# Second expert layer of a decoder: dense experts over all tokens, or each routed expert over its own rows

## The reference, cut to what matters

```python
gates = softmax(x @ router_w); idx1 = argmax(gates); idx2 = argmax(gates * (1 - mask1))
pos1 = cumsum(mask1) - mask1;                 mask1 *= pos1 < capacity
pos2 = cumsum(mask2) - mask2 + sum(mask1);    mask2 *= pos2 < capacity
g1, g2 = g1 / max(g1 + g2, eps), g2 / max(g1 + g2, eps)
expert_in = einsum('nec,nh->ech', dispatch, x)          # 560 rows for each of 8 experts
hmid = silu(einsum('ech,ehf->ecf', expert_in, w1) + b1)  # 128 -> 512
expert_out = einsum('ecf,efh->ech', hmid, w2) + b2       # 512 -> 128
y = einsum('nec,ech->nh', combine, expert_out)
out = y + 0.1 * (silu(x @ sw1 + sb1) @ sw2 + sb2)
```

## Time and profile before

| | us |
|---|---|
| median of 3 runs | 1636.73 |
| profiled execution, first to last instruction (span) | 1638.0 |
| last stage, from its first load to the end | 1428.1 to 1638.0 |
| nine experts' matmuls, first to last | 1437.4 to 1633.7 |

### The profile page before, as it was taken

The page is one execution under the profiler, slowest core; times in us unless marked ns, Lnnn a source line. Parts: engine busy times, 40 slices in busy tenths (PEclk is TensorE's granted clock), DMA queues, the critical chain, the costliest instruction groups (busy, mean ns, idle before and its releaser), DMA issues. The chain is left out here.

```text
span 1638.0 us, 45036 instructions
## 1 busy us (share of the span) xinstructions
PE 1531.2 (93%) x16356; PEld 1187.5 (72%) x16356; DVE 1108.0 (68%) x1746; ACT 897.3 (55%) x1421; POOL 705.6 (43%) x757
## 2 busy tenths in 40 slices
PE   8988999989999987789999999999999999889998
PEld 4445676679989655467777777777777777678887
DVE  4334545677787468467777777777777777367777
ACT  5454332432222347346666666666666666567776
POOL 2200000577877456443444433444433444066665
PEclk9779999999999999799999999999999999989999
DMA  2064984131110000466655556655556654212211
GB/s 78 21 171 122 241 253 120 39 127 42 64 42 23 0 2 2 104 153 153 151 131 130 130 135 150 150 126 130 128 141 150 145 127 112 56 42 75 75 60 45
DMA packets 55699, 169.74 MB, mean 104 GB/s; under 512 B 13761, under 2 KB 27425, under 8 KB 55617
## 3 DMA queue, kind: packets, MB, share of 16 engines
q1 hardware_dynamic: 52928, 156.83, 38.4%
q10 hardware_dynamic: 2688, 11.78, 2.4%
HBM read 90.80 MB, written 1.29 MB: 56 GB/s over the span
## 5 line engine op out<-in xcount | busy, mean ns | idle before, releaser
L1993 DVE TENSOR_REDUCE hat_tops<-banks 128x1 f32<-128x500 f32 x672 | 441.8, 676 | 151.6 <-PE banks L1738 151.4
L1866 ACT ACTIVATE hat_pb<-banks 125x896 f32<-125x896 f32 x384 | 340.2, 916 | 226.7 <-PE banks L1757 222.5
L1738 PE MATMUL banks<-hat_kh,hat_qm 128*128 128x500 f32 x672 | 298.4, 461 | 3.7 <-DVE hat_tops L1993 3.4
L1757 PEld LDWEIGHTS banks<-hat_q,hat_k 128*125 128x125 f32 x1536 | 219.3, 188 | 74.9 <-issue 32.6
L1757 PE MATMUL banks<-hat_q,hat_k 128*125 128x224 f32 x1536 | 250.3, 286 | 16.4 <-ACT hat_pb L1866 9.1
L1935 POOL CAST hat_kh<-hat_kf 128x500 fp32r<-128x500 f32 x96 | 58.3, 607 | 403.6 <-ACT hat_kf L1879 389.3
L1748 PE MATMUL banks<-hat_pb,hat_vs 125*27 125x168 f32 (+1 forms) x6144 | 166.9, 261 | 0.1
L1748 PEld LDWEIGHTS banks<-hat_pb,hat_vs 125*27 125x27 f32 (+1 forms) x6144 | 132.0, 98 | 44.1 <-issue 24.4
L1311 ACT ACTIVATE ffn_rg<-banks 128x448 f32<-128x448 f32 x128 | 69.7, 545 | 164.4 <-PE banks L1244 164.3
L1738 PEld LDWEIGHTS banks<-hat_kh,hat_qm 128*128 128x128 f32 x672 | 127.5, 191 | 41.0 <-DVE hat_tops L1993 25.5
L2247 DVE TENSOR_TENSOR moe_hl<-moe_hf,moe_hh 128x448 fp32r<-128x448 f32 x128 | 108.5, 887 | 42.2 <-POOL moe_hh L2139 41.5
(11 more groups left out here) (293 smaller groups left out, 3055.8 us busy)
## 6 DMA issues: line engine op xcount, KB each, us to landing
hat_k<-hat_kh SPq DMA_DIRECT2D x256, 187.5 KB, 4.7
hat_ct<-ctxT SPq DMA_DIRECT2D x32, 750.0 KB, 6.2
hat_k<-hat_kl SPq DMA_DIRECT2D x128, 187.5 KB, 4.5
ctx_cx<-ctx SPq DMA_DIRECT2D x32, 672.0 KB
ctx_cd<-ctxT ACTq DMA_DIRECT2D x15, 750.0 KB, 5.4
ffn_cb<-expert_weights SPq DMA_DIRECT2D x8, 896.0 KB, 4.4
moe_cb<-expert_weights SPq DMA_DIRECT2D x8, 896.0 KB, 6.6
moe_raw<-Mw SPq DMA_DIRECT2D x18, 256.0 KB, 3.0
```

Source lines behind the costliest of these rows:

```text
L1738: peak_out.inc(nc.tensor.matmul(g.bank(PK + m % 2)[:, 0:SB], qm[u][:].rearrange("p h i -> p (h i)")[:, r * 128:r * 128 + 128], kh[u][:, c ...
L1757: mm = nc.tensor.matmul(g.bank(2 * (t % 2) + j // 2)[0:SW, (j % 2) * QW:(j % 2 + 1) * QW], k3[u][:, j, t * SW:(t + 1) * SW], q3[u][:, j, : ...
L1866: exped.inc(nc.scalar.activation(pb[t % 6][:].rearrange("p (n i) -> p n i", n=2), g.ps[0:SW, 2 * (t % 2):2 * (t % 2) + 2, 0:2 * QW], ACT.E ...
L1993: peaked.inc(v.tensor_reduce(tops[:, r, n:n + 1], g.bank(PK + m % 2)[:, 0:SB], AX_X, ALU.max))
```

## The change

`experts_silu` and its helper go; `experts1` is written anew. SLOTS = 8 x 560 = 4480 rows of XW = 130 words (128 features, one word for the token's number, one spare) lie in DRAM (`slot_rows`), and 2 x 1792 rows of 128 (`token_rows`) for the results. Both are cleared by SP in the first block of the causal attention.

- The normalized tokens are turned to rows (14 transposes on PE), kept by ACT, doubled by POOL for the second choice, and given their numbers. `Route` works out the slot of each token and choice on DVE; each of 2 x 14 tiles of 128 rows is sent to its slots by an indirect DMA issued on POOL.
- Meanwhile the shared expert runs over all tokens as before, with a ring of 6 tiles and a lag of 4; POOL makes its first four remainders, DVE the other twelve, after it has worked out the slots. DVE adds a tenth of its output to `xt` (`mix`).
- SP loads the 560 rows of an expert, PE turns them (`turn`), ACT and DVE split them, and the expert runs over 4 tiles of 560 columns, each as two halves of 280 (6 matmuls up, 6 down). DVE adds the bias, PE turns the result back (`turn_out`), and POOL sends it to its tokens by 5 indirect DMAs of 112 rows (`send`), whose indices lie in the rows that came (`rows`, three buffers). Six sets of split weights are kept, made by POOL, for three of them by ACT and DVE.
- At the end SP loads both results of each token, PE sums them with matmuls against diagonal matrices of the shares (`lots`), and DVE adds them to `xt`.

```diff
+SLOTS = E * CAPACITY
+XW = D + 2
@@ causal_attention, first block
+            @block.sync
+            def _(sp):
+                sp.wait_ge(emptied, 2)
+                sp.dma_start(g.slot_rows.rearrange("(n p) c -> p n c", p=128), spread(g.empty[:], 1, SLOTS // 128)).then_inc(cleared, 16)
+                sp.dma_start(g.token_rows.rearrange("(n p) c -> p n c", p=128), spread(g.empty[:, 0:D], 1, 2 * TT)).then_inc(cleared, 16)
+                sp.wait_ge(cleared, 32)
...
+                nc.gpsimd.memset(g.empty[:, 0:D], 0.0).then_inc(emptied, 1)
+                nc.gpsimd.memset(g.empty[:, D:XW], 1.0).then_inc(emptied, 1)
@@ Route(Choice)
+    def take(self, dve, k):
+        self.candidates(dve, k, (self.sc, self.rest)[k])
+        self.step(dve, v.tensor_reduce(self.row[:, 7, :], self.tmp[:], AX_X, ALU.max))
+        v.tensor_tensor(self.hot[:, k], self.tmp[:], self.wide(7), ALU.is_equal).then_inc((self.one, self.two)[k], 1)
...
+    def place(self, dve, bank, k):
+        dve.wait_ge(self.tallied, k + 1)
...
+        for n in (1, 2, 4, 8):
+            v.tensor_copy(b[:, 0:n], a[:, 0:n]).then_inc(self.stepped, 1)
+            v.tensor_tensor(b[:, n:TT], a[:, n:TT], a[:, 0:TT - n], ALU.add).then_inc(self.stepped, 1)
...
+        v.tensor_scalar(self.slot[:, k], self.row[:, 4, :], float(SLOTS), None, ALU.add).then_inc(self.slotted, 1)
@@ experts1, SP
+                    if s == SETS - 1:
+                        sp.wait_ge(sent_all, 16 * 2 * TT)
+                        for e in range(3):
+                            sp.dma_start(rows[e][:], g.slot_rows[...]).then_inc(rows_in[e], 16)
+                for e in range(3, E):
+                    sp.wait_ge(out_sent[e - 3], 16 * 5)
+                    sp.dma_start(rows[e % 3][:], g.slot_rows[...]).then_inc(rows_in[e % 3], 16)
+                for e in range(E - 3, E):
+                    sp.wait_ge(out_sent[e], 16 * 5)
+                for i, (a, b) in enumerate(GROUPS):
+                    if i >= 2:
+                        sp.wait_ge(joined, i - 1)
+                    for k in range(2):
+                        sp.dma_start(back[i % 2][:, k, 0:b - a, :], source).then_inc(back_in[i % 2], 16)
@@ experts1, POOL
+                for s in range(3):
+                    split(s)
+                for c in range(CH):
+                    pool.wait_ge(x_high, c + 1)
+                    nc.gpsimd.tensor_tensor(chunk(xl, c), chunk(g.xn, c), chunk(xh, c).bitcast(F32), ALU.subtract).then_inc(x_low, 1)
...
+                for k in range(2):
+                    pool.wait_ge(pick.slotted, k + 1)
+                    for t in range(TT):
+                        nc.gpsimd.indirect_dma_start(out=g.slot_rows, out_offset=bass.IndirectOffsetOnAxis(ap=pick.slot[:, k, t:t + 1], axis=0),
+                                                     in_=sent[:, k, t, :], in_offset=None, bounds_check=SLOTS - 1, oob_is_err=False).then_inc(sent_all, 16)
+                def send(e):
+                    pool.wait_ge(out_kept, e + 1)
+                    for n in range(5):
+                        nc.gpsimd.indirect_dma_start(out=g.token_rows, out_offset=bass.IndirectOffsetOnAxis(ap=rows[e % 3][:, n, D:D + 1].bitcast(mybir.dt.int32), axis=0),
+                                                     in_=ow[e % 2][:, n, :], in_offset=None, bounds_check=2 * NT - 1, oob_is_err=False).then_inc(out_sent[e], 16)
+                for e in range(E):
+                    j = FT * e
+                    pool.wait_ge(made, j + 1)
+                    if e >= 1:
+                        pool.wait_ge(down, j + 1 - FT)
+                    pool.sem_inc(rounding, 1)
+                    nc.gpsimd.tensor_copy(ring(hh, j), ring(hf, j)).then_inc(high_pool, 1)
+                    if e >= 2:
+                        send(e - 2)
+                    if e in (0, 2, 3):
+                        split((6, None, 7, 8)[e])
+                send(E - 2)
+                send(E - 1)
@@ experts1, PE
+                def turn(e):
+                    pe.wait_ge(rows_in[e % 3], 16 * (e // 3 + 1))
...
+                turn(0)
+                for e in range(E):
+                    up_part(e, 0)
+                    if e:
+                        down_part(e - 1, 2)
+                    up_part(e, 1)
+                    if e + 1 < E:
+                        turn(e + 1)
+                    if e:
+                        down_part(e - 1, 3)
+                    up_part(e, 2)
+                    down_part(e, 0)
+                    up_part(e, 3)
+                    if e:
+                        turn_out(e - 1)
+                    down_part(e, 1)
...
+                for i, (a, b) in enumerate(GROUPS):
+                    pe.wait_ge(back_in[i % 2], 32 * (i // 2 + 1))
@@ experts1, DVE
+                pick.place(dve, g.bank(3), 0)
+                pick.place(dve, g.bank(2), 1)
...
+                for j in range(POOLED, UN):
+                    low_shared(j)
+                    if j in (4, 8, 12):
+                        rest(2 + j // 4)
+                    if j == 6:
+                        pick.shares(dve)
+                    if j % FT == 1 and j >= 9:
+                        mix((j - 9) // FT)
```

More of the change, by code:

```diff
@@ L2075, in experts_silu @@
[L2075 to L2086, removed]
+        raw = [sb(f"raw{u}", [128, 2, F]) for u in range(RAWS)]
+        wh, wl = ([sb(f"{n}{u}", [128, 2, F], F32R) for u in range(SETS)] for n in ("wh", "wl"))
+        xh, xl = sb("xh", [128, NT], F32R), sb("xl", [128, NT], F32R)
@@ new lines, in experts1, with high_of @@
+        out_sent = [sem(f"out_sent{e}") for e in range(E)]
+        back_in = [sem(f"back_in{u}") for u in range(2)]
+        joined, added, stored = sem("joined"), sem("added"), sem("stored")
+        ring0 = lambda t, j: t[:, (j % RING) * CW:(j % RING + 1) * CW]
+        ring = lambda t, j: t[:, (j % FT) * CAPACITY:(j % FT + 1) * CAPACITY]
+        f128 = lambda f: slice(f * 128, f * 128 + 128)
+        def high_of(n):
+            return (high_pool, n // FT + 1) if n % FT == 0 else (high_act, n - n // FT)
@@ L2089, in _ @@
             def _(sp):
[L2090 to L2100, removed]
@@ new lines, in down_part @@
+                def down_part(e, f):
+                    n, s = FT * e + f, (e + 1) % SETS
+                    if f == 0 and e >= 1:
+                        pe.wait_ge(biased_out, e)
+                    hs, count = high_of(n)
+                    pe.wait_ge(hs, count)
+                    pe.wait_ge(low, n + 1)
+                    for k in range(2):
+                        half = slice(k * HALF, (k + 1) * HALF)
+                        mm = three(nc, g.bank(k)[:, 0:HALF], wh[s][:, 1, f128(f)], wl[s][:, 1, f128(f)], ring(hh, n)[:, half], ring(hl, n)[:, half],
+                                   start=(f == 0), stop=(f == FT - 1))
+                    mm.then_inc(down, 1)
@@ new lines, in _ @@
+                keep_high(0)
+                for e in range(E):
+                    for f in range(FT):
+                        n = FT * e + f
+                        act.wait_ge(up, n + 1)
+                        if n >= FT:
+                            act.wait_ge(low, n + 1 - FT)
+                        nc.scalar.activation(ring(hf, n).rearrange("p (k x) -> p k x", k=2), g.ps[:, 4 + 2 * (n % 2):6 + 2 * (n % 2), 0:HALF],
+                                             ACT.Silu, bias=b1[:, e + 1, f:f + 1]).then_inc(made, 1)
+                        if n:
+                            round_up(n - 1)
+                        if f == 1 and e + 1 < E:
+                            keep_high(e + 1)
@@ L2284, in _ @@
[L2284 to L2297 removed]
+                pick.probabilities(dve)
```

459 lines of the change are left out of this document (294 added, 165 removed).

## The result

The changed kernel takes 1672.35 us (median, 1669.57 to 1675.4) beside 1635.85 us for the kernel before (1630.55 to 1640.17): a ratio of 1.0229, 95% interval 1.0199 to 1.0259. The forecast was 1659 us, in a range of 1612 to 1700: slower, as it said, and 13 us more than it said. The profiled execution took 1673.79 us, of which 1672.0 is its span (1638.0 before).

A forecast was written before the change was run, and what follows sets the result against it. The prediction took PE's matmul columns to bound each expert before; after, serial sends delay the routed start about 31 us, five ring turns take 104, and the end reaches 1660: +22 us on 1638.0, so 1659 us, range 1612 to 1700.

The forecast's parts named there:

- The price of an issue: POOL's indirect transfers, 68 on the path: 1.2 us each, bounds 0.33 and 1.89, break-even 0.88.
- rival B: The 68 issues on POOL: each well below 0.88 us, say 0.6, 41 us less, 1618 us; chance 0.15.
- Rival C: POOL held up while issuing beside DVE's work: 0.4 us more per issue, 27 us, 1686 us; chance 0.20.
- Start of the stage: Router and sends before the routed experts: first routed matmul at 1501.8, about 31 us later than before.
- The ring: Three row buffers: loading expert e+1's rows waits for e-2's results to land; 20.8 us a turn, five times 104.
- the half clock: PE's work behind each idle stretch of the ring: 7.5 us taken, between 6.0 at full clock and 11 at half.
- The end: After up(7,0) at 1622.8: 15 sends to 1642.5, landing, loads and joins of four token groups, output; ends at 1660.
- PE's busy time: Whole kernel, profile after: PE busy some 1440 us in a longer span.
- The earlier stage: Clearing two DRAM tables (4.2 MB) in causal attention's first block: hidden, taken as 0, with 5 us kept as possible.
- Rival D: The ring doesn't close and the loop runs at PE's 8 us: 64 us less, 1595 us; chance 0.05.

The follow-up runs named there:

- the sends first: Changed kernel with three row buffers; on POOL the result issues of expert e-2 stand ahead of expert e's first cast: 1673.68 us, ratio 1.0204.
- the one turn of the experiment: Changed kernel plus 11 unread 448-column matmuls on constants in PE's idle time of turns 2 to 6: 1668.98 us, ratio 1.018.
- an open ring: Changed kernel with eight row buffers instead of three, so no load of rows waits for results to land: 1619.96 us, ratio 0.9882.
- the weights early: Eight row buffers, plus the last three experts' raw weights loaded before the wait for sends and POOL's last three splits moved earlier: 1612.36 us, ratio 0.9841.

## Why the prediction was right, and where it was 13 us short

- **The price of an issue** was the step on which the sign hung: taken 1.2 us, bounds 0.33 and 1.89, break-even 0.88. It is 1.27 and 1.24 (0.97 or 0.94 busy and 0.30 between). That the nearest row was POOL's own subtract on 128 partitions, and not SyncE's plain issue, was the right choice; rival B falls. That it came within 0.07 us is in part luck: the price is 0.97 or 0.94 of work and a gap of 0.30, and the prediction had no gap in it. For 68 issues the difference is 28 x 0.07 + 40 x 0.04, some 3 to 4 us. The Trainium skill, page "DMA: Bandwidth & Descriptors", section "Latency and other measured facts", has about 1 us for the emission; the busy part of 0.94 to 0.97 agrees with it, but the pitch, by which a row of issues goes, has 0.30 more.
- **Rival C**, 0.4 us more on each, is right in kind and a third of its size. Six of the first 14 sends have it, and their mean pitch is 1.49 us: 2.6 us in all. In the ring DVE does stand idle for most of a turn, as the prediction said against it, but not when POOL's cast and first issue come: the two multiplies put 2.2 and 2.0 us on two casts, and DVE's remainders 0.3 to 0.5 us on the first issue of each group. With one issue near the end that is some 9 us by the durations (an estimate: their sum over 0.97, 0.94 and 0.65 us), where rival C had 27 and the forecast nothing. The Trainium skill, page "SBUF — State Buffer", section "Who interferes with whom", has VectorE's two-port copies block GpSimd, and two-input operations contend with its reads. The long issues and casts here stood beside the second kind, multiplies and subtracts with both inputs in SBUF.
- **Start of the stage.** Slots of the first choice at 1460: the first issue is at 1460.15. Last send done at 1493.7 forecast, 1498.4 measured (2.1 us of price, 2.6 of DVE). The landing was taken at 1.9 us behind the issue and is 1.3 (2.30 from its start); turn and rounding were 2.5 and are 3.1, as PE's clock is at half after 25 us of idleness. First routed matmul 1501.8 forecast, 1506.47 measured: 4.7 us short. The shared expert ends at 1478, not 1484; 20 us of sends lie bare behind it.
- **The ring.** That it closes, where, and by which links was right: five gaps of PE of 10.3 to 12.9 us, each ended by moe_rows, and 106.2 us instead of 104 from the first Silu of expert 2 to that of expert 7. The last three turns take 20.4 to 20.5 us, 0.3 to 0.4 less than the sum of the links; the first two take 22.4 and 22.5, with a multiply of DVE in each that lengthens POOL's cast by 2 us and had no term in the prediction. Two links were sized or placed wrong. I had POOL's cast in the ring; the chain names it, but the experiment with the sends first shows that DVE's copy ends so late that the cast adds only 0.26 us. And I had 1.5 us a turn for the half clock (7.5 instead of 6.0 us). The stretch takes 8.2 us at a granted clock of 0.70 and 6.3 at 1.00, in the one turn of the experiment that was granted it: 1.9 us.
- **The end.** Last issue forecast to start near 1641.3 and be done at 1642.5; it is done at 1652.75. 4.7 of the 10.25 us come from the start, 1.2 from experts 0 and 1, 2.2 from the ring, the rest from the last 15 issues: 0.4 of price, 0.6 for two of them that DVE made longer, and 1.1 because POOL sat idle 1.4 us before those of expert 6; I had them back to back. From there to the end 17.5 us were forecast and 19.25 are measured: the first group's join takes 3.77 us, not 1.9, at a granted clock of 0.50, and from the last join to the end it is 4.1, not 3; the landing is 0.8 shorter, and the last two joins take 2.96 together, at the full clock (3.3 forecast). Sum 12.0 us on the profiled span; the remaining 1.3 is that before's span lay above its median and after's does not.
- **PE's busy time** was to be 1440 and is 1462.6. The matmul of 280 columns is 0.13 us at full clock as worked out, but many of them ran at half, 0.23 us, behind each wait.
- **The earlier stage** at nothing: right, and the waits show the cover.
- **Rival D** was rightly small, and by the experiments its price was overrated: an open ring gives 1620 us, not 1595, since POOL's splits and the waits between the engines come next.

So PE's busy time fell by 68.6 us, and waits came in: 25 us ahead of the first routed expert and 10 to 13 us in each of five turns. With one more row buffer the kernel is faster than the one before (1622 us), and with eight and the weights early it takes 1612.

## What to carry to other kernels

Before sparse work replaces dense work, follow the ring of its buffers: who must land before which load may start, and how far behind the loop that send is issued. If that takes longer than the dense step did, nothing is won, however much arithmetic goes, and one more buffer may be worth more than all of it. Price indirect transfers by their number on POOL, not by bytes. And a link that the chain of waits names may only stand in front of another that ends at the same time: its own price shows only when it is taken away. Read the clock in the stretch that counts: the mean over a whole turn held the filling matmuls and hid that the work behind the wait still ran near the half clock.

## What the runs showed of the hardware

- An indirect issue holds POOL for 0.97 us (128 rows) or 0.94 (112), with 0.30 between two; rows that are skipped don't make it cheaper (at least 2688 of 4480 slots empty: still 0.94 and 0.30). Results landed 2.0 to 2.8 us after the start of their issue.
- An issue or a cast of POOL that starts while DVE is in an operation with both inputs in SBUF is longer by what is left of it, less some 0.12 us (behind the large multiply also by the subtract that followed at once, among the sends not): sends 1.30 to 1.44 us instead of 0.97, casts 2.85 and 2.64 instead of 0.65. In the kernel with the sends first, the first issue of a group that met no such operation (at 1564.75) took 0.95, three others 1.39 to 1.41. A fifth issue took 3.70 though DVE's multiply began 0.22 us behind its start, so when in an issue POOL can be held is not settled.
- Behind a wait of 10 to 13 us PE's work up to the next Silu took 7.7 to 8.2 us at a granted clock of 0.80 to 0.69, and 6.3 us in the one turn with 1.00. Filling matmuls that ended 2 to 5 us before the work came kept the clock full in one turn of five only.
- Clearing 4.2 MB by two broadcast stores (2275 and 1792 KB) took 18.5 us to landing, beside other work.
